# Softmax sums of an attention stage: two products of 64 columns and one reciprocal, or four products of 32 columns and eight reciprocals

## The reference

```
logits = q @ k^T            # per batch and head, q scaled by 1/8
attn   = softmax(logits, axis=-1)
out    = attn @ v           # then a projection with Wp, plus bp
```

## Time and profile before

| | |
|---|---|
| median of three runs | 1919.21 us |
| the profiled execution | 1928.73 us, span 1926.7 us |
| PE busy | 1858.0 us, 96% |
| DVE busy | 1222.8 us, 63% |
| POOL busy | 1344.6 us, 70% |
| ACT busy | 860.3 us, 45% |
| mean granted TensorE clock | 0.978 of full speed |

### The profile page before, as it was taken

How to read it: one execution, slowest core, us unless ns; L and a number is a source line. 1 busy time by engine, 2 the same in 40 slices (tenths; PEclk the granted TensorE clock), 3 DMA queues, 4 the chain that set the end, 5 groups by cost and what they waited for, 6 DMA issues and landing times.

```text
span 1926.7 us, 30738 instructions
## 1 busy us (share of the span) xinstructions
PE 1858.0 (96%) x11400; PEld 1189.7 (62%) x11400; DVE 1222.8 (63%) x2147; ACT 860.3 (45%) x1102; POOL 1344.6 (70%) x719
## 2 busy tenths in 40 slices
PE   7899999999999999999999999999999999989997
PEld 5555555555665565556665555556655554788886
DVE  5566566666666657667666667667666577754565
ACT  3344444444435444343444543444354433554674
POOL 1688777788667867797668676986678676650564
PEclk9899999999999999999999999999999999977999
DMA  4310000002221000023211000121110101732330
GB/s 142 86 34 18 23 18 23 18 23 83 88 62 42 12 14 23 29 78 94 55 38 41 17 23 18 45 78 50 31 58 23 39 12 45 211 110 69 127 132 34
DMA packets 132142, 104.24 MB, mean 54 GB/s; under 512 B 58140, under 2 KB 118684, under 8 KB 130972
## 3 DMA queue, kind: packets, MB, share of 16 engines
q1 hardware_dynamic: 128924, 93.81, 16.3%
q0 software_dynamic: 3072, 8.46, 1.2%
HBM read 69.15 MB, written 29.43 MB: 51 GB/s over the span
## 4 chain that ended last, share of the span: by engine, by line
PE 84%; DVE 5%; POOL 4%; issue 3%; ACT 1%; DMA 1%; SPq 0%; another core or an unknown queue 0%; POOLq 0%; DVEq 0%; ACTq 0%
PE score_ps L1127 22%; PE av_ps L1141 21%; PE spare_ps L1090 9%; PE spare_ps L1106 8%; PE spare_ps L1083 5%; PE h_ps L1680 4%; PE y_ps L1709 4%; PE spare_ps L441 4%; PE spare_ps L1152 3%; POOL prob_sum L1011 3%; DVE max_of L1283 1%; PE spare_ps L490 1%; PE spare_ps L465 1%; PE y_ps L1696 1%; PE h_ps L1696 0%
## 5 line engine op out<-in xcount | busy, mean ns | idle before, releaser
L1011 POOL TENSOR_TENSOR prob_sum<-prob_sum,probs 128x1024 f32<-128x1024 f32 (+1 forms) x384 | 906.2, 2360 | 203.3 <-ACT probs L1227 171.3
L1283 DVE TENSOR_REDUCE max_of<-spare_ps 128x1 f32<-128x512 f32 x1024 | 656.8, 683 | 346.1 <-PE spare_ps L1106 335.2
L1227 ACT ACTIVATE probs<-score_ps 128x1024 f32<-128x1024 f32 x512 | 502.6, 1025 | 688.3 <-PE score_ps L1127 667.1
L1141 PE MATMUL av_ps<-probs,v 128*64 128x512 f32 x2048 | 489.5, 603 | 3.0 <-ACT probs L1227 1.6
L1141 PEld LDWEIGHTS av_ps<-probs,v 128*64 128x64 f32 x2048 | 129.8, 136 | 241.0 <-issue 220.1
L1007 POOL TENSOR_TENSOR prob_sum<-probs 128x1024 f32<-128x1024 f32 (+1 forms) x64 | 150.2, 2347 | 146.0 <-ACT probs L1227 145.9
L1106 PE MATMUL spare_ps<-k_hi,q_hi 64*128 64x512 f32 x1024 | 229.8, 442 | 22.6 <-DVE max_of L1283 21.9
L1106 PEld LDWEIGHTS spare_ps<-k_hi,q_hi 64*128 64x128 f32 x1024 | 99.4, 185 | 226.7 <-issue 190.7
L1127 PE MATMUL score_ps<-q_hi,k_hi 64*128 64x512 f32 x1024 | 211.3, 407 | 1.1 <-DVE o_in L1333 0.9
L1127 PE MATMUL score_ps<-shift_rows,ones 64*128 64x512 f32 x1024 | 205.3, 395 | 0.0
L1127 PE MATMUL score_ps<-q_lo,k_hi 64*128 64x512 f32 x1024 | 204.9, 394 | 0.0
(11 more groups left out here) (249 smaller groups left out, 2406.7 us busy)
## 6 DMA issues: line engine op xcount, KB each, us to landing
o_transposed<-o_out SPq DMA_DIRECT2D x64, 256.0 KB, 2.0
v<-in_L_ffn_W_dram SPq DMA_DIRECT2D x16, 1024.0 KB
o_in<-o_transposed SPq DMA_DIRECT2D x28, 512.0 KB, 4.0
w_raw<-in_L_attn_Wq_dram SPq DMA_DIRECT2D x64, 64.0 KB, 2.3
w_raw<-in_L_attn_Wk_dram SPq DMA_DIRECT2D x64, 64.0 KB, 2.2
wv_raw<-in_L_attn_Wv_dram SPq DMA_DIRECT2D x32, 128.0 KB, 3.1
shift_rows<-neg_rows SPq DMA_DIRECT2D x256, 1.0 KB
x<-in_x_dram SPq DMA_DIRECT2D x4, 1024.0 KB, 5.8
```

What stands on the lines that cost most here:

```text
L1011: pool.tensor_tensor(out, out, probs[:, n % RING, heads], ALU.add).then_inc(prob_added, 1)
L1141: last = pe.matmul(av_ps[hd * E:(hd + 1) * E, :], v[:, quad % 2, kt, 2 * first_head + hd, :], probs[:, n % RING, hd, :], start=(kt == 0), ...
L1227: act.activation(probs[:, n % RING], score_ps[n % 2][:, :, :], ACT.Exp).then_inc(probs_ready, 1)
L1283: dve.tensor_reduce(max_of[:, u % 2, kh, j, hd:hd + 1], bank[:, :], AX.X, ALU.max).then_inc(pass_read, 1)
```

## The change

The ones have 32 columns in place of 64, and each head's 512 queries are taken in two halves of 256. Four products fill four strips of 32 partitions of the bank's first 256 columns: head 0's first half, its second half, head 1's first half, its second half. The first transposition is over 256 columns instead of 512. Each strip of `sums` then holds the sums of one half of one head in 8 columns, and the layout of `inverse` stays as it was; so each strip's 8 columns are inverted twice, into both strips of its head: eight reciprocals of 32 partitions x 8. None of them waits for another; the second transposition waits for all eight and is unchanged.

```diff
     BLOCK = 32
+    HALF = BANK // 2
+    HEAD_HALVES = ((0, 0), (0, 1), (1, 0), (1, 1))
...
+    def strip(hd, half):
+
+        return slice((2 * hd + half) * BLOCK, (2 * hd + half + 1) * BLOCK)
...
-                for hd in range(2):
-                    last = pe.matmul(bank[hd * E:(hd + 1) * E, :], ones[:, 0:E], prob_sum[:, u % 2, hd, :],
-                                     start=True, stop=True)
+                for hd, half in HEAD_HALVES:
+                    last = pe.matmul(bank[strip(hd, half), 0:HALF], ones[:, 0:BLOCK],
+                                     prob_sum[:, u % 2, hd, half * HALF:(half + 1) * HALF], start=True, stop=True)
...
-                dve.transpose(sums[:, :], bank[:, :]).then_inc(sum_turned, 1)
+                dve.transpose(sums[:, 0:HALF], bank[:, 0:HALF]).then_inc(sum_turned, 1)
...
                 dve.wait_ge(sum_turned, u + 1)
-                dve.reciprocal(inverse[:, :], sums[:, 0:BANK:BLOCK]).then_inc(recip_done, 1)
-                dve.wait_ge(recip_done, u + 1)
+                blocks = HALF // BLOCK
+                for hd, half in HEAD_HALVES:
+                    for other in range(2):
+                        dve.reciprocal(inverse[strip(hd, other), half * blocks:(half + 1) * blocks],
+                                       sums[strip(hd, half), 0:HALF:BLOCK]).then_inc(recip_done, 1)
+                dve.wait_ge(recip_done, 2 * len(HEAD_HALVES) * (u + 1))
```

## The result

The changed kernel is slower: 1986.03 us (median of four runs, 1982.75 to 1987.54) against 1919.51 (a fourth run of the kernel before took 1922.2); ratio 1.0343, 95% interval 1.0326 to 1.0359. That is +66.5 us where +51 was forecast, inside the range. The profiled execution took 1986.38 us, span 1984.3 us. Span against span is only +57.6, because the profiled execution of before ran 9 us above its other runs; the last block took about 7 us more in it (273.9 us at a mean granted clock of 0.90, against 267.1 at 0.92). The code of that block is the same in every run here, and over the twelve profiled executions it took from 264 to 274 us, so differences of a few us between two single executions say nothing.

A forecast was written before the change was run, and what follows sets the result against it. PE was taken as the bound, with DVE only just in time in odd units. Odd units +33.2, even sums -8.0, even recips +25.1 and the end +0.8 make +51 us on 1919.2: 1970 us, range 1928 to 1990.

The forecast's parts named there:

- DVE's part: DVE's work per unit: first transposition 0.27 us shorter, eight reciprocals 1.37 us longer than the one.
- PE's part: PE's sum matmuls: 0.43 us saved on columns, less an added change of the array's form, so 0.25 saved per sum.
- the step at 951.14: PE's next step in the profiled odd unit, waiting for DVE's last read; forecast 1.07 us later.
- the added change of form: The array changes tiling once more around each sum, since av stays at 64 columns; taken as 0.18 us.
- First transposition: DVE's transposition of the sums, over 256 columns instead of 512: 0.445 us instead of 0.712.
- Spacing of the reciprocals: Start to start among DVE's eight reciprocals: 0.203 us, the record's length, giving +1.37 us per unit.
- rival of overlapping reciprocals: The eight reciprocals overlap on DVE, 0.12 us apart: +17 us in all, 1936 us; chance 0.20.
- Odd units: In 31 odd units DVE's longer path delays PE by 1.07 us each, +33.2 us; PE's saving is worth nothing.
- Recips of even units: Reciprocals at the half-step's end delay DVE's read of the next half-step's opening pass: +25.1 us.
- the nine units where nothing gives: Even units where DVE was still busy ahead of recip: the full 1.37 us lost in each, +12.3 us.
- the thirteen like unit 8: Even units with 0.71 us of room around the read behind recip: 0.66 us lost in each, +8.6 us.
- the other nine: Even units with more or less room around the read behind recip: 0.2 to 0.9 us each, +4.2 us.

The follow-up runs named there:

- one_recip: The changed kernel with one reciprocal of 128 x 16 in place of the eight, so outputs are wrongly scaled; 1909.2 us, ratio 0.9923.
- before_eight: The kernel before with its one reciprocal cut into eight of 32 x 8, products and transposition unchanged; 1964.04 us, ratio 1.0202.
- same_strip: The changed kernel with its eight reciprocals all reading strip 0 and writing strip 0, result incomplete; 1929.64 us, ratio 1.0033.
- out_moves: As same_strip, but the eight write strips 0, 1, 2, 3 twice over while all read strip 0; 1983.57 us, one run.
- in_moves: As same_strip, but the eight read strips 0, 1, 2, 3 twice over while all write strip 0; 1985.45 us, one run.
- after_late_recip: The changed kernel with recip of odd units moved from ahead of the half-step's third pass to behind its fourth; 1962.61 us, ratio 1.0198.
- after_both_moved: The changed kernel with recip moved behind the fourth pass in odd units and ahead of the bite in even ones; 1936.61 us, ratio 1.0076.

## Why the prediction was right, point by point

**Direction and mechanism held.** PE bound, DVE only just in time in the odd units: one_recip and before_eight take the two parts of the change apart, and DVE's part alone makes the loss.

**PE's part:** -0.25 forecast, -0.26 measured in the even units, nothing in the odd ones, where the sum step is shorter too, but the step at 951.14 still waits for DVE. Four strips do run side by side, 0.24 us from set to set. With 0.43 us for the columns, the rest of the sum's 0.57 and the 0.03 on the pass make 0.17 for the added change of form, against 0.18 assumed.

**First transposition:** 0.445 forecast, 0.445 measured.

**Spacing of the reciprocals:** I took the end of the record, 0.203. It is 0.225: the record itself is shorter than a 128 x 8 one (0.195), but the next starts 0.03 behind it. That is +1.52 us per unit, not +1.37, and this is the first term that was mis-sized. The choice of 0.203, between two values, came near, but no row stood behind it. The rival of overlapping reciprocals fell because of the strips alone, as same_strip shows.

**Odd units:** 1.07 each forecast; with 1.52 the same working gives 1.22; 1.23 measured in the unit shown, 31 x 0.15 = 5 us of the miss.

**Recips of even units:** the same 0.15 in 31 places is 4 to 5 us more: 25.1 becomes 29.8. The classes held: low clock aside, the nine units where nothing gives lose about 1.53 us each, the thirteen like unit 8 lose 0.74, the other nine 3.9 in all.

**The second mis-sized term is one that the sum didn't have: the granted clock.** In the units up to 58, eight stretches at half of full speed (the lower level, 1.2 GHz, instead of 2.4) are in the trace after, and one in the trace before. In unit 16 the stretch ran at 0.55 where it had run at 1.00. Five of the eight are behind recips of even units (16, 28, 32, 44, 48), where PE stood still for 2.4 or 3.7 us (0.6 or 2.2 before); the one before is in unit 44 too. Three are in odd units (25, 41, 57), behind a standstill of 1.15 us that all odd units but the last have. A v bite takes 2.49 us from the start of its first matmul to that of its last instead of 1.38 there. Against like units without such a stretch, each of the seven new ones costs 1.4 to 1.8 us: 11 us in all.

The low clock comes with the late reads: out_moves and in_moves show seven and eight such stretches at the same places, one_recip two, and after_late_recip, with the odd recips moved away, none in odd units. Nor does the length of a standstill decide it alone: after_both_moved keeps 2.52 us in units 16, 32 and 48, and only unit 32 has a low stretch behind it. What decides it stays open.

**Waits of the sums for POOL** were left out as unchanged, 9.8 us. Those were the waits of PE's weight loads alone; with PE's own there were 15.9 us in 8 places, and 12.1 in 6 after. In units 30 and 46 PE now comes later relative to POOL and waits 1.4 us less in each: this worked against the loss.

**Put together.** PE runs the same steps in the same order in both traces, so the start of every `av` after can be set against its start before. From the first `av` to the last normalising, these two executions differ by 65.9 us:

| us | forecast | measured |
|---|---|---|
| odd units | +33.2 | +37.3 |
| sums of even units | -8.0 | -8.7, and -3.4 by shorter waits for POOL |
| recips of even units | +25.1 | +27.4 |
| the last two units | +0.8 | +2.1 |
| low clock, taken out of the rows above | none | +11.2 |
| sum | +51 | +65.9 |

The paths and the waits were as forecast. Of the miss of 15 us between these two executions, 11 are the clock and 6 the longer spacing; the waits for POOL took 3.4 back. The medians differ by 66.5 us. The clock's share is of one execution of each kernel.

## What to carry to other kernels

Where two engines take turns at a few buffers, the busy share says nothing of room: DVE was 65% busy, and of the 1.25 us added to its run of back-to-back work in an odd unit 1.23 reached PE. Before one operation on all partitions is cut into several on 32, count how many neighbours change strips on either side: those don't overlap. And it pays to try a step that isn't urgent at a place where its engine waits for another one, not between a result and the read that frees a bank. Measure each such move: in the kernel before it gave 10 us in the even units and cost 7 in the odd ones.

## What was not expected

- The price of a strip change against none: spacings of 0.22 to 0.23 against 0.074 us for 32 x 8 reciprocals; one changed side is enough.
- Of neighbours that overlap, the later record is itself shorter, 0.145 against 0.192 us.
- Behind some standstills of PE, of 1.15 to 3.7 us, the matmuls ran at half the clock for a while, 1.4 to 1.8 us on top. Others as long had no such stretch behind them.
- In the kernel before, one word moved by a few steps makes it 0.5% faster in the even units and 0.35% slower in the odd ones.
